# Dense stage of a four-layer residual kernel: separate PSUM banks per sum, 512-column products, outputs put together on VectorE

## The chip, the core and the metric

The kernel runs on one core of a Trainium2 chip. The metric is the device time of one execution in microseconds (us), the median of three runs. TensorE (PE) is the matrix engine and PEld its weight loads, VectorE is DVE, ScalarE is ACT, GpSimd is POOL and SyncE is SP.

## What is computed

x has 128 sequences of 64 channels and 1024 positions, in float32. Four layers follow each other, each added to its input:

```
x = x + L0(x)   # a long convolution of each channel, masked by the sequence's length
x = x + L1(x)   # each sequence: a 64x64 mix of the channels, one of 16 chosen by an index
x = x + L2(x)   # x @ W2.T + bias + (x @ A2.T) @ B2.T, the rank-16 pair A2, B2 one of 32
x = x + L3(x)   # x @ W3.T + 0.5 * (x @ A3) @ B3.T, rank 32, A3 one of 5
```

L2 and L3 work along the 1024 positions. The kernel multiplies their dense weights into one 1024 x 1024 matrix and keeps what is low in rank (both adapters and the bias) as a separate product of small rows.

## The kernel before

There are three stages. The preparation, to about 190 us, builds the combined weights and the tables. The convolution follows, to about 580 us. The **dense stage** does L1, L2 and L3, and the change lies there; outside it only the places of some weight columns move.

A tile is 128 rows: two sequences of 64 channels. The dense stage takes two tiles at a time, a **pair**: 32 pairs, of which the first and the last are written out and the rest run in a loop on every engine (`over_pairs`). A pair is a 2 x 2 block matrix a11, a12, a21, a22 (128 rows x 512 positions each), and the combined weight is 2 x 2 blocks of 512 x 512. Winograd's form of Strassen's method makes the four output blocks from seven products M1 to M7 instead of eight:

```
y11 = M1 + M2                  y12 = M1 + M6 + M5 + M3
y21 = M1 + M6 + M7 + M4        y22 = M1 + M6 + M7 + M5
```

The signs lie in the operands and weights, and all four take low-rank rows on top. Every operand is held as a high and a low part in a reduced format of float32, so a product is three passes over four chunks of 128 positions: 12 steps. A step of 512 output columns was issued as two matmuls of 256. M1, M5, M2 and M4 are **wide**: they also form 96 columns for the adapters (x times the A tables), so their two matmuls have 256 and 352 columns. M6, M3 and M7 are **plain**.

The order of a pair's work on TensorE is written out in `pair` of the tensor block: M1, M5, M2, M4 (with a transpose, `turn`, of the adapters' rows in its middle), `adapters` (a small product), a `quarter` (the L1 mix of a quarter of the next pair, eight matmuls at L1573), M6 with the second `turn` in its middle, `low_rank` for y11, `adapters`, a quarter, M3, a quarter, M7, three `low_rank`, the last quarter. Each `low_rank` is four matmuls of 256 columns, two accumulating steps for two halves. The engines' orders are fixed by hand as well; all waits are semaphores.

PSUM has 8 banks of 512 float32 columns. Before the change, two sums share a bank by halves: P (M1, then M6 and M7 added onto it) and S (M2) share one, R (M5, then M3) and V (M4) another (`PS_SHARED`, `RV_SHARED`). The rest:

- ScalarE copies sums out into `y_out` on the way: M1 (L1386), M5 (L1391), M1 + M6 after the first `low_rank` (L1395), M1 + M6 + M7 (L1404). The first two overwrite `y_out` of the previous pair and so wait for its two stores (`y_stored`).
- VectorE adds a second PSUM sum onto each: y11 (L1541), y12 (L1548), y22 (L1553), y21 (L1555). It also makes the operands of the next products (L1466 to L1470 xs1 and its parts, L1512 to L1523), chooses the next rows by sequence length (L1442, L1447) and gathers the adapters' columns (`h_rows`, L1481 and L1485, which adds the parts of two products; `h_columns`, L1490).
- ScalarE issues the stores of the output rows (L1408 first tile, L1415 second), SP the loads.
- M1 of the next pair waits for y22's addition, since it writes the bank of P.

```
L1621  pe.wait_ge(a11_lo, n + 1)
L1622  pe.wait_ge(h_lo[0], n + 1)
L1623  ready(pe, y22_added, n)
L1624  product(xa11, M1, PS_SHARED, P_OWN, ALL, True).then_inc(m1_done, 1)
```

Of the kernel before, what the change touches and what calls it, by code (L numbers as in the profile page):

```python
# [39 lines left out]
H_AT = (HB, 0, HB, 0)  # L40
D_AT = (0, KR, 0, KR)


def program(nc, x, xt_in, steps, cond, adapter, labeler, log_dt, ssm_c, log_a_real, a_imag, ssm_d,
# [276 lines left out]
    def count_in(k, u, bufs=BUFS):  # L321
# [30 lines left out]
    m1_done, m5_done, m2_done, m4_done, lr11_done, m7_done, rv_done, p_done = (  # L352
        sem(f"{n}_done") for n in ("m1", "m5", "m2", "m4", "lr11", "m7", "rv", "p"))
    p_copied, r_copied, u2_copied, u3_copied = (sem(f"{n}_copied") for n in ("p", "r", "u2", "u3"))
    h_part, hrow_ready, turned, hc_ready, adapted, hs_hi, hs_lo = (
        sem(n) for n in ("h_part", "hrow_ready", "turned", "hc_ready", "adapted", "hs_hi", "hs_lo"))
    y11_added, y12_added, y22_added, y21_added = (sem(f"{n}_added") for n in ("y11", "y12", "y22", "y21"))
# [908 lines left out]
    with nc.Block() as block:  # L1266
# [89 lines left out]
        def _(act):  # L1356
# [22 lines left out]
            def pair(n, last_one):  # L1379
# [6 lines left out]
                copy(halves(y_out[0][:, 0:HB]), of_p, ACT.Copy).then_inc(p_copied, 1)  # L1386
# [4 lines left out]
                copy(halves(y_out[1][:, HB:T]), of_r, ACT.Copy).then_inc(r_copied, 1)  # L1391
# [3 lines left out]
                copy(halves(y_out[0][:, HB:T]), of_p, ACT.Copy).then_inc(u2_copied, 1)  # L1395
# [164 lines left out]
        def _(pe):  # L1560
# [59 lines left out]
            def pair(n, last_one):  # L1620
# [44 lines left out]
                if not last_one:  # L1665
                    quarter(n + 1, 3)
# [41 lines left out]
```

## Time and profile before

| | |
|---|---|
| median of 3 runs | 1503.09 us (1501.48 to 1505.19) |
| the profiled execution: span | 1500.9 us, first to last instruction |
| TensorE busy | 1456.2 us, 97% |
| VectorE busy | 1114.5 us, 74% |
| ScalarE busy | 631.1 us, 42% |
| GpSimd busy | 117.3 us, 8% |
| granted TensorE clock, mean | 0.995 of 2.4 GHz |

The three runs are timed without the profiler; the profiled execution is known by its span. Busy shares are means over stages with different limits, and a busy TensorE is not one without stalls: matmuls are pipelined, so the record of one (about 280 ns for 256 columns) overlaps the next, and what a matmul costs is the time from its start to the next one's start.

### The profile page before, as it was taken

To read this page: it belongs to the slowest core of one execution; us is meant where nothing else is said; L and a number is where in the kernel's file an instruction comes from. 1 tells how busy PE (TensorE), PEld (TensorE's weight loads), DVE (VectorE), ACT (ScalarE), POOL (GpSimd) and SP (SyncE) were. 2 spreads that over 40 slices of the span, in tenths; PEclk is the share of its full clock that TensorE was granted. 3 is DMA by queue.
4 is the path that set the end of the run, shared out by engine and by line. 5 is a ranking of instruction groups with operands and counts; after the bars stand their busy time and mean duration, and the time that the engine had idled before them with its cause. 6 is when DMAs were issued, how large, how long until landed. Compare 5 with 4: busy or idle time off the path is not lost.

```text
span 1500.9 us, 33974 instructions
## 1 busy us (share of the span) xinstructions
PE 1456.2 (97%) x10624; PEld 1404.1 (94%) x10624; DVE 1114.5 (74%) x2330; ACT 631.1 (42%) x1249; POOL 117.3 (8%) x188
## 2 busy tenths in 40 slices
PE   6989989999999997999999999999999999999998
PEld 5877879999999997999999999999999999999998
DVE  7975388888888885777777777777777777777674
ACT  4331256665656562343343343343343343334332
POOL 3451210000000000000000000000000000000000
PEclk9999999999999998999999999999999999999999
DMA  8133168888888877456556556556556656645652
GB/s 306 33 134 99 42 220 277 274 277 273 274 272 274 273 242 228 128 158 198 146 157 196 145 163 191 145 160 195 142 151 193 160 147 179 177 147 166 191 147 78
DMA packets 121380, 276.16 MB, mean 184 GB/s; under 512 B 23897, under 2 KB 64349, under 8 KB 118689
## 3 DMA queue, kind: packets, MB, share of 16 engines
q1 hardware_dynamic: 111308, 241.28, 54.1%
q10 hardware_dynamic: 10038, 34.46, 5.8%
q8 instruction: 18, 0.29, 0.1%
q14 instruction: 16, 0.13, 0.0%
HBM read 200.72 MB, written 74.95 MB: 184 GB/s over the span
## 4 chain that ended last, share of the span: by engine, by line
PE 87%; DVE 6%; DMA 3%; POOL 1%; issue 1%; ACT 1%; SPq 0%; DVEq 0%; ACTq 0%; POOLq 0%
PE ps L1602 23%; PE ps L1603 23%; PE ps L1234 13%; PE ps L1573 8%; PE ps L1245 6%; PE ps L1136 4%; PE ps L1225 3%; PE ps L1610 2%; PE ps L1612 2%; PE ps L1237 2%; DMA out<-y_out 1%; PE ps L1584 1%; DVE p L810 1%; DVE b3t L906 1%; DMA b_d<-b_last 1%
## 5 line engine op out<-in xcount | busy, mean ns | idle before, releaser
L1602 PE MATMUL ps<-weights,xs 128*128 128x256 f32 x1536 | 397.4, 289 | 0.0
L1603 PE MATMUL ps<-weights,xs 128*128 128x256 f32 (+1 forms) x1536 | 388.8, 292 | 0.0
L1602 PE MATMUL ps<-weights,xa 128*128 128x352 f32 (+1 forms) x1152 | 329.2, 313 | 4.6 <-ACT y_out L1386 1.3
L1603 PE MATMUL ps<-weights,xa 128*128 128x256 f32 (+1 forms) x1152 | 322.7, 295 | 0.0
L1602 PEld LDWEIGHTS ps<-weights,xs 128*128 128x128 f32 x1536 | 292.5, 190 | 0.0
L1603 PEld LDWEIGHTS ps<-weights,xs 128*128 128x128 f32 x1536 | 292.4, 190 | 0.0
L1602 PEld LDWEIGHTS ps<-weights,xa 128*128 128x128 f32 x1152 | 217.0, 188 | 10.7 <-issue 10.7
L1234 PE MATMUL ps<-toep,ut 128*128 128x512 f32 (+2 forms) x1152 | 226.7, 342 | 0.0
L1603 PEld LDWEIGHTS ps<-weights,xa 128*128 128x128 f32 x1152 | 217.2, 189 | 0.0
L1234 PEld LDWEIGHTS ps<-toep,ut 128*128 128x128 f32 x1152 | 194.3, 189 | 16.6
L1362 ACT ACTIVATE a<-ps 128x512 f32<-128x512 f32 x128 | 76.5, 598 | 274.2 <-PE ps L1573 259.5
L1573 PE MATMUL ps<-m_gath,x_in 128*128 128x128 f32 x1024 | 137.2, 278 | 8.9 <-DVE x_in L1455 8.9
L1573 PEld LDWEIGHTS ps<-m_gath,x_in 128*128 128x128 f32 x1024 | 127.0, 195 | 9.3 <-DVE x_in L1455 9.3
L1136 PE MATMUL ps<-p,staged 128*128 128x512 f32 x480 | 111.2, 393 | 6.9 <-POOL staged L595 4.8
L752 ACT ACTIVATE ut<-xt 128x896 fp32r<-128x896 f32 x64 | 61.0, 953 | 135.2 <-PE ps L1245 129.2
L1136 PEld LDWEIGHTS ps<-p,staged 128*128 128x128 f32 x480 | 90.9, 190 | 26.7 <-issue 5.2
L1334 POOL COPY m_gath<-mix 64x64 f32 x128 | 46.1, 360 | 823.0 <-PE ps L1573 719.9
L1245 PE MATMUL ps<-toep,ut 128*128 128x256 f32 x768 | 107.3, 289 | 0.0
L1447 DVE COPY_PREDICATED x_in<-late,x_nat 128x512 f32<-128x512 uint16 x124 | 92.5, 746 | 18.9 <-DVE late L1442 18.9
L1245 PEld LDWEIGHTS ps<-toep,ut 128*128 128x128 f32 x768 | 95.8, 190 | 0.0
L422 ACT ACTIVATE weights<-tab 128x128 fp32r<-128x128 f32 (+1 forms) x256 | 71.4, 353 | 26.6 <-DVE tab L429 26.5
L1059 DVE TENSOR_TENSOR ut<-xt,ut 128x896 fp32r<-128x896 f32 x64 | 69.9, 1092 | 16.3 <-ACT ut L752 16.3
(223 smaller groups left out, 2182.3 us busy)
## 6 DMA issues: line engine op xcount, KB each, us to landing
lags<-kern_d SPq DMA_DIRECT2D x64, 512.0 KB, 5.2
xt<-in_xt SPq DMA_DIRECT2D x64, 512.0 KB, 6.0
x_d<-yo SPq DMA_DIRECT2D x64, 512.0 KB, 3.2
x_nat<-in_x SPq DMA_DIRECT2D x64, 512.0 KB, 3.9
x_in<-x_d SPq DMA_DIRECT2D x64, 512.0 KB, 5.6
out<-y_out ACTq DMA_DIRECT2D x63, 512.0 KB, 5.8
tab<-a_d SPq DMA_DIRECT2D x128, 128.0 KB, 2.1
stack<-b_d SPq DMA_DIRECT2D x126, 128.0 KB, 4.1
```

Source lines behind the costliest of these rows:

```text
L422: ins = nc.scalar.activation(to, of, ACT.Copy)
L752: copy(ut[u % 2][:, 0, 0:SPLIT], xt[u % BUFS][:, 0:SPLIT], ACT.Copy).then_inc(ut_hi, 1)
L1059: tt(ut[u % 2][:, 1, 0:SPLIT], xt[u % BUFS][:, 0:SPLIT], f(ut[u % 2][:, 0, 0:SPLIT]), ALU.subtract).then_inc(ut_lo, 1)
L1136: ins = mm(t[:, cols], staged[n % 2][:, a, c, :], p3[:, c, b, cols], start=c == a == b == 0, stop=c == K8 - 1 and a == 1)
L1234: mm(y[:, half * HB + i * P:(half + 1) * HB], xs[:, a, half * half_t + i, :], tp[:, b, 0:HB - i * P], start=i == a == b == 0, stop=False)
L1245: ins = mm(y[:, to:to + QT], xs[:, a, i, :], tp[:, b, at_col:at_col + QT], start=False, stop=i == half_t - 1 and a == 1)
L1334: ins = nc.gpsimd.tensor_copy(m_gath[v][rows, b * C:(b + 1) * C], mix[rows, bass.ds(s, 1), :].squeeze(1))
L1362: ins = copy(raw[:], mixing, ACT.Copy)
L1447: nc.vector.copy_predicated(x1_in[v][:, cols], late[:], x_nat[v][:, cols]).then_inc(chosen[v], 1)
L1573: ins = mm(acc[:, bank, i * P:(i + 1) * P], x1_in[v][:, c * P:(c + 1) * P], m_gath[v][:], start=True, stop=True)
L1602: mm(left[0], x_part, left[1], start=first and is_wide, stop=end, skip_group_check=True)
L1603: ins = mm(right[0], x_part, right[1], start=first and is_wide and H_AT[m] > 0, stop=end, skip_group_check=True)
```

## The change

- **PSUM banks.** Six banks for the sums of products, none shared: `S_LEFT`, `S_RIGHT` hold M1 and M2 (y11), `V_LEFT`, `V_RIGHT` hold M5 and M4, `P_BANK` M6 and then M7, `Q_BANK` M3. In S and V the 96 adapter columns stand behind the right half, so all four wide products run 256 then 352 columns (M2 and M4 were 352 then 256), and the adapters' columns of two products add up in PSUM: `h_rows` loses its additions.
- **Plain products** write one bank of 512 columns: one matmul of 512 for two of 256. The low-rank rows of y12 and y22 do the same.
- **Outputs.** ScalarE copies M1 (now S), M5 (now V) and later y11 as a whole. VectorE forms M1 - M5 and M1 + M5 from the copies (`pair_sums`) and adds P, V and Q to them from PSUM (V holds M5 + M4 by then, so y21 starts from M1 - M5). The two copies of U2 and U3 on ScalarE are gone.
- **Order and waits.** On TensorE the last quarter moves ahead of the last `low_rank`, which waits for VectorE's read of P after M7 (`u3_read`). M1 waits for y11's copy, M6 for y22, M3 for y12. ScalarE copies a12 without waiting for M7, and the second store waits for y22 as well as y21. In the last pair the y11 half is stored by itself.

The core of the diff, the banks first:

```diff
-    S_OWN, PS_SHARED, P_OWN, V_OWN, RV_SHARED, R_OWN, SMALL_BANK, MIX_BANK = range(8)
+    S_LEFT, S_RIGHT, V_LEFT, V_RIGHT, P_BANK, Q_BANK, SMALL_BANK, MIX_BANK = range(8)
```

ScalarE's part of a pair:

```diff
-                copy(halves(y_out[0][:, 0:HB]), of_p, ACT.Copy).then_inc(p_copied, 1)
+                copy(halves(y_out[0][:, 0:HB]), of_s, ACT.Copy).then_inc(m1_copied, 1)
...
-                copy(halves(y_out[1][:, HB:T]), of_r, ACT.Copy).then_inc(r_copied, 1)
+                copy(halves(y_out[1][:, HB:T]), of_v, ACT.Copy).then_inc(m5_copied, 1)
...
                 act.wait_ge(lr11_done, n + 1)
-                copy(halves(y_out[0][:, HB:T]), of_p, ACT.Copy).then_inc(u2_copied, 1)
+                act.wait_ge(pair_sums, 2 * n + 2)
+                copy(halves(y_out[0][:, 0:HB]), of_s, ACT.Copy).then_inc(y11_copied, 1)
...
-                act.wait_ge(m7_done, n + 1)
-                copy(halves(y_out[1][:, 0:HB]), of_p, ACT.Copy).then_inc(u3_copied, 1)
-                if not last_one:
                     take(n + 1, 3, a12, xa12)
                 act.wait_ge(y12_added, n + 1)
...
                 else:
+                    act.wait_ge(y22_added, n + 1)
                     act.dma_start(out_rows[bass.ds(2 * n + 1, 1)].squeeze(0), y_out[1][:]).then_inc(y_stored[1], 16)
```

VectorE's part:

```diff
+                dve.wait_ge(m1_copied, n + 1)
+                dve.wait_ge(m5_copied, n + 1)
+                tt(y_out[1][:, 0:HB], y_out[0][:, 0:HB], y_out[1][:, HB:T], ALU.subtract).then_inc(pair_sums, 1)
+                tt(y_out[1][:, HB:T], y_out[0][:, 0:HB], y_out[1][:, HB:T], ALU.add).then_inc(pair_sums, 1)
                 dve.wait_ge(m2_done, n + 1)
                 h_rows(n, 0)
...
-                dve.wait_ge(u2_copied, n + 1)
-                tt(halves(y_out[0][:, 0:HB]), halves(y_out[0][:, 0:HB]), of_s, ALU.add).then_inc(y11_added, 1)
+                dve.wait_ge(m6_done, n + 1)
+                dve.wait_ge(pair_sums, 2 * n + 2)
+                tt(y_out[0][:, HB:T], y_out[1][:, HB:T], of_p, ALU.add).then_inc(u2_read, 1)
```

TensorE, the plain products and the order of a pair:

```diff
+            def plain_product(operand, m, bank, chunks, opens):
+
+                for i in chunks:
+                    for a, b in PASSES:
+                        ins = mm(acc[:, bank], operand[:, a, i, :], plain(i, b, m), start=opens and i == a == b == 0,
+                                 stop=i == K4 - 1 and a == 1, skip_group_check=True)
+                return ins
...
+            PIECES_S = ((acc[:, S_LEFT, 0:HALF], HALF), (acc[:, S_RIGHT, 0:HALF], HALF))
+            PIECES_P, PIECES_Q = ((of_p, HB),), ((of_q, HB),)
...
-                ready(pe, y22_added, n)
-                product(xa11, M1, PS_SHARED, P_OWN, ALL, True).then_inc(m1_done, 1)
+                ready(pe, y11_copied, n)
+                wide_product(xa11, M1, S_LEFT, S_RIGHT, ALL, True).then_inc(m1_done, 1)
...
-                pe.wait_ge(y11_added, n + 1)
-                product(xs3, M7, PS_SHARED, P_OWN, ALL, False).then_inc(m7_done, 1)
-                low_rank(0, HB, acc[:, RV_SHARED, LEFT], acc[:, R_OWN, LEFT])
+                pe.wait_ge(u2_read, n + 1)
+                plain_product(xs3, M7, P_BANK, ALL, False).then_inc(m7_done, 1)
+                low_rank(0, HB, PIECES_Q)
...
-                low_rank(1, 0, acc[:, V_OWN, RIGHT], acc[:, RV_SHARED, RIGHT]).then_inc(rv_done, 1)
-                pe.wait_ge(u3_copied, n + 1)
-                low_rank(1, HB, acc[:, PS_SHARED, LEFT], acc[:, P_OWN, LEFT]).then_inc(p_done, 1)
+                low_rank(1, 0, PIECES_V).then_inc(qv_done, 1)
                 if not last_one:
                     quarter(n + 1, 3)
+                pe.wait_ge(u3_read, n + 1)
+                low_rank(1, HB, PIECES_P).then_inc(p_done, 1)
```

TensorE at the end of a pair, before (stack and hs are the low-rank operands, m_gath and x_in the quarter's, xa_157 the operand of M1):

```order
L1610 MATMUL ps<-stack_175,hs_182 128x256 [waits u3_copied]
L1612 MATMUL ps<-stack_175,hs_182 128x256
L1610 MATMUL ps<-stack_175,hs_182 128x256
L1612 MATMUL ps<-stack_175,hs_182 128x256
L1573 MATMUL ps<-m_gath_189,x_in_188 128x128 [waits quarter_read,chosen0]
L1573 MATMUL ps<-m_gath_189,x_in_188 128x128 x3
L368 UNCONDITIONAL_BRANCH
L368 ISA
L1602 MATMUL ps<-weights,xa_157 128x256 [waits y22_added,h_lo0,x_a11_lo]
```

The same place after the change:

```order
L1601 MATMUL ps<-weights,xs_163 128x512 x11
L1610 MATMUL ps<-stack_174,hs_181 128x512 x2
L1610 MATMUL ps<-stack_175,hs_182 128x256 [waits stack_landed1,hs_lo]
L1610 MATMUL ps<-stack_175,hs_182 128x256 x3
L1574 MATMUL ps<-m_gath_189,x_in_188 128x128 [waits quarter_read,chosen0]
L1574 MATMUL ps<-m_gath_189,x_in_188 128x128 x3
L1610 MATMUL ps<-stack_175,hs_182 128x512 [waits u3_read]
L1610 MATMUL ps<-stack_175,hs_182 128x512
L366 UNCONDITIONAL_BRANCH
L366 ISA
L1593 MATMUL ps<-weights,xa_157 128x256 [waits y11_copied,h_lo0,x_a11_lo]
```

The last low-rank rows stand behind the quarter instead of ahead of it, and M1 waits for y11's copy instead of y22's addition. M7 and two of the low-rank groups are matmuls of 512 columns.

VectorE ahead of the first transpose, before (late and x_in belong to the choice of the next rows, hrow is what TensorE transposes):

```order
L1442 TENSOR_SCALAR late<-ramp,lens_cols 128x256 [waits chosen0,x_landed0,x1_landed0]
L1442 TENSOR_SCALAR late<-ramp,lens_cols 128x256
L1447 COPY_PREDICATED x_in_188<-late,x_nat_177 128x512 [waits late_made]
L1481 COPY hrow_191<-ps 64x48 [waits m2_done]
L1481 COPY hrow_191<-ps 64x48
L1485 TENSOR_TENSOR hrow_191<-hrow_191,ps 64x48 [waits h_part]
L1485 TENSOR_TENSOR hrow_191<-hrow_191,ps 64x48
L1490 COPY hc_179<-ps 64x128 [waits turned]
```

and after:

```order
L1446 TENSOR_SCALAR late<-ramp,lens_cols 128x256 [waits chosen0,x_landed0,x1_landed0]
L1446 TENSOR_SCALAR late<-ramp,lens_cols 128x256
L1451 COPY_PREDICATED x_in_188<-late,x_nat_177 128x512 [waits late_made]
L1525 TENSOR_TENSOR y_out_173<-y_out_172,y_out_173 128x512 [waits m5_copied,m1_copied]
L1526 TENSOR_TENSOR y_out_173<-y_out_172,y_out_173 128x512
L1481 COPY hrow_191<-ps 64x48 [waits m2_done]
L1481 COPY hrow_191<-ps 64x48
L1486 COPY hc_179<-ps 64x128 [waits turned]
```

The two sums of copied products stand between the choice and the adapters' rows, and the rows' two additions are gone.

## Rows read from the trace of the kernel before

**Rows 1.** The page: busy time, share of the span, instructions of each engine.

```profile
PE 1456.2 (97%) x10624; PEld 1404.1 (94%) x10624; DVE 1114.5 (74%) x2330; ACT 631.1 (42%) x1249; POOL 117.3 (8%) x188
```

**Rows 2.** By stretches: length, engines' busy us, granted clock, DMA share, GB/s.

```profile
800.00:900.00 100.00, 99.70 (x792) 99.01 (x791) 73.08 (x183) 39.13 (x85) 4.49 (x12) 1.00 0.56 160
```

**Rows 3.** Timeline, TensorE, first M1 in pairs 1 and 31 (start, us).

```profile
615.64 0.35 PE L1602 MATMUL ps<-weights,xa 128*128 128x256 f32 x1
...
1470.88 0.35 PE L1602 MATMUL ps<-weights,xa 128*128 128x256 f32 x1
```

**Rows 4.** Timeline, TensorE: a quarter, then M7 (second and following matmuls).

```profile
809.28 1.06 PE L1573 MATMUL ps<-m_gath,x_in 128*128 128x128 f32 x8
...
810.30 0.28 PE L1603 MATMUL ps<-weights,xs 128*128 128x256 f32 x1
...
813.05 0.28 PE L1610 MATMUL ps<-stack,hs 128*128 128x256 f32 x1
```

**Rows 5.** Timeline, TensorE in the preparation, equal matmuls merged.

```profile
120.91 65.57 PE L1136 MATMUL ps<-p,staged 128*128 128x512 f32 x288 [0.60 <-DVE lora_out L1025]
```

**Rows 6.** Groups by line and form, TensorE, 512 columns (busy us, mean ns).

```profile
L1234 PE MATMUL ps<-toep,ut 128*128 128x512 f32 x384 | 115.1, 407 | 0.0
L1136 PE MATMUL ps<-p,staged 128*128 128x512 f32 x480 | 111.2, 393 | 6.9 <-POOL staged L595 4.8 <-DVE raw L932 1.6 <-DVE lora_out L1025 0.6
```

**Rows 7.** Timeline, VectorE and TensorE, end of the pair before 815.64.

```profile
812.88 0.69 DVE L1470 TENSOR_TENSOR xs<-s,xs 128x512 fp32r<-128x512 f32 x1
814.21 0.69 DVE L1548 TENSOR_TENSOR y_out<-y_out,ps 128x512 f32<-128x512 f32 x1 [0.63 <-PE ps L1612]
814.48 1.06 PE L1573 MATMUL ps<-m_gath,x_in 128*128 128x128 f32 x8
814.81 0.68 DVE L1553 TENSOR_TENSOR y_out<-y_out,ps 128x512 f32<-128x512 f32 x1
...
815.83 0.33 PE L1603 MATMUL ps<-weights,xa 128*128 128x352 f32 x1
```

**Rows 8.** Timeline, ScalarE, the next pair: copies of M1, M5 and M1 + M6.

```profile
821.04 0.60 ACT L1386 ACTIVATE y_out<-ps 128x512 f32<-128x512 f32 x1 [1.74 <-DMA out<-y_out]
...
824.44 0.60 ACT L1391 ACTIVATE y_out<-ps 128x512 f32<-128x512 f32 x1 [2.28 <-DMA out<-y_out]
...
833.88 0.60 ACT L1395 ACTIVATE y_out<-ps 128x512 f32<-128x512 f32 x1 [2.37 <-PE ps L1612]
```

**Rows 9.** Timeline, TensorE, the same pair: steps of M1, then M2 into M4.

```profile
816.00 0.28 PE L1602 MATMUL ps<-weights,xa 128*128 128x256 f32 x1
...
816.55 0.28 PE L1602 MATMUL ps<-weights,xa 128*128 128x256 f32 x1
...
825.37 0.32 PE L1602 MATMUL ps<-weights,xa 128*128 128x352 f32 x1
...
825.65 0.32 PE L1602 MATMUL ps<-weights,xa 128*128 128x352 f32 x1
```

**Rows 10.** Timeline, VectorE and TensorE, the same pair, up to the first transpose (L1579).

```profile
824.85 0.75 DVE L1447 COPY_PREDICATED x_in<-late,x_nat 128x512 f32<-128x512 uint16 x1 [0.15 <-DVE late L1442]
825.85 0.42 DVE L1481 COPY hrow<-ps 64x48 f32<-64x48 f32 x2 [0.25 <-PE ps L1603]
826.31 0.41 DVE L1485 TENSOR_TENSOR hrow<-hrow,ps 64x48 f32<-64x48 f32 x2
...
827.33 0.27 PE L1579 MATMUL ps<-ident,hrow 128*128 128x128 f32 x1
```

**Rows 11.** By line: landing of the first store (L1408), then the second (L1415).

```profile
DMA to landing us min/median/max: 2.7/5.3/5.9
...
DMA to landing us min/median/max: 5.8/7.6/8.9
```

**Rows 12.** Timeline, a late pair: M5's copy on ScalarE, then M4 on TensorE.

```profile
1451.67 0.60 ACT L1391 ACTIVATE y_out<-ps 128x512 f32<-128x512 f32 x1 [2.85 <-DMA out<-y_out]
...
1452.41 0.40 PE L1602 MATMUL ps<-weights,xa 128*128 128x352 f32 x1 [0.25 <-ACT y_out L1391]
```

More of the change, by code:

```diff
@@ L351, in program @@
     h_hi, h_lo = [sem(f"h_hi{v}") for v in range(2)], [sem(f"h_lo{v}") for v in range(2)]
[L352 to L357, printed above, removed]
+    m1_done, m5_done, m2_done, m4_done, m6_done, lr11_done, m7_done, qv_done, p_done = (
+        sem(f"{n}_done") for n in ("m1", "m5", "m2", "m4", "m6", "lr11", "m7", "qv", "p"))
+    m1_copied, m5_copied, y11_copied = (sem(f"{n}_copied") for n in ("m1", "m5", "y11"))
+    hrow_ready, turned, hc_ready, adapted, hs_hi, hs_lo = (
+        sem(n) for n in ("hrow_ready", "turned", "hc_ready", "adapted", "hs_hi", "hs_lo"))
+    pair_sums, u2_read, u3_read = sem("pair_sums"), sem("u2_read"), sem("u3_read")
+    y12_added, y22_added, y21_added = (sem(f"{n}_added") for n in ("y12", "y22", "y21"))
     PAIRS = TILES // 2
@@ L373, in h_table @@
     def h_table(half, m):
-        start = (half * 4 + m) * WIDE + H_AT[m]
+        start = (half * 4 + m) * WIDE + HB
         cols = weights[:, :, start:start + KR]
@@ L1472, in h_rows @@
             def h_rows(n, v):
-                own, other = ((P_OWN, H_END), (S_OWN, H_FRONT)) if v == 0 else ((R_OWN, H_END), (V_OWN, H_FRONT))
-                parts = []
+                bank = (S_RIGHT, V_RIGHT)[v]
                 for b in range(2):
-                    rows, cols = slice(b * C, (b + 1) * C), slice(b * R2, b * R2 + R2 + R3)
-                    parts.append((hrow[v][rows, cols], rows, slice(b * (R2 + R3), (b + 1) * (R2 + R3))))
-                first, second = acc[:, own[0], own[1]], acc[:, other[0], other[1]]
-                for b, (to, rows, cols) in enumerate(parts):
-                    ins = nc.vector.tensor_copy(to, first[rows, cols])
-                ins.then_inc(h_part, 1)
-                dve.wait_ge(h_part, 2 * n + v + 1)
-                for to, rows, cols in parts:
-                    ins = tt(to, to, second[rows, cols], ALU.add)
+                    rows, start = slice(b * C, (b + 1) * C), H_COLS + b * (R2 + R3)
+                    ins = nc.vector.tensor_copy(hrow[v][rows, b * R2:b * R2 + R2 + R3], acc[rows, bank, start:start + R2 + R3])
                 ins.then_inc(hrow_ready, 1)
@@ L1584, in adapters, with wide_product @@
                 mm(acc[:, SMALL_BANK, P:2 * P], c_gath[v][:], hc[v][:], start=True, stop=True).then_inc(adapted, 1)
[L1586 removed]
+            def wide_product(operand, m, left, right, chunks, opens):
                 for i in chunks:
                     for a, b in PASSES:
[L1590 to L1603 removed]
@@ new lines, in wide_product @@
+                        start, end = opens and i == a == b == 0, i == K4 - 1 and a == 1
+                        x_part, w = operand[:, a, i, :], wide(i, b, m)
+                        mm(acc[:, left, 0:HALF], x_part, w[:, 0:HALF], start=start, stop=end, skip_group_check=True)
+                        ins = mm(acc[:, right, 0:HALF + KR], x_part, w[:, HALF:WIDE], start=start, stop=end, skip_group_check=True)
+                return ins
[4 more added lines that the diff above has]
+                                 stop=i == K4 - 1 and a == 1, skip_group_check=True)
+                return ins
```

93 lines of the change are left out of this document (42 added, 51 removed).

## Prediction

> **What bounds the kernel now.** I read the page's engine totals, then the table by stretches, then single instructions. TensorE is busy 97% of the span [rows 1], and in the dense stage, from 614 us on, over 99% at full clock, with VectorE at 73% and ScalarE at 39% [rows 2]. One turn of the dense loop (a pair) takes (1470.88 - 615.64) / 30 = 28.51 us [rows 3]. So the time there is the length of TensorE's instruction stream plus its stalls, and work on other engines counts only where TensorE waits for it. The duration in a row of a matmul is latency, since matmuls overlap; what counts is start to start. Two things in the stream can be shortened: the 256-column matmuls of M6, M3 and M7 with their low-rank rows, and one stall at each pair's end, which the busy share hides.
>
> **The merge of 256 to 512 columns.** From 810.30 to 813.05 stand 23 matmuls of 256 columns of M7, so one takes 2.75 / 23 = 119.6 ns [rows 4]. The kernel has matmuls of 512 columns in the same arithmetic, accumulating into one bank, in its preparation: 288 in 65.57 us, less some 0.17 us of latency of the last, give 227.1 ns each [rows 5]. Two of 256 cost 239.1 ns, so a merge saves 12 ns. A pair merges 36 in M6, M3 and M7 and 4 in the low-rank additions: 40 x 12 = 0.48 us, times 32 pairs = **15.4 us**. The convolution's matmuls of 512 columns have a mean record of 407 ns against 393 ns in the preparation [rows 6]; read as 14 ns more of pitch, this would be 241 ns, and the merge would gain nothing. That is the lower end, 0; I take 15.4 because the preparation's rows have the same passes and the same width into one bank. The Trainium skill (TensorE: Matmul & The Clock Gate, Back-to-back issue gap) puts the isolated spacing at N/2.4 + 2.5 ns, by which a merge would save only 2.5 ns, some 3 us in all; the trace does not agree at 256 columns, where the page would have 109.2 ns and the rows have 119.6.
>
> **The stall at the pair's end.** Inside a pair, from the first matmul of a quarter (eight matmuls at L1573) to the second matmul of the next product is 810.30 - 809.28 = 1.02 us [rows 4]; at the pair's end it is 815.83 - 814.48 = 1.35 us [rows 7]. The 0.33 us more are a wait: M1 waits for y22's addition (L1553), which ends at 814.81 + 0.68 = 815.49 [rows 7]. The change lets M1 wait for y11's copy, which follows lr11, some 10 us earlier (a copy stands at that place now, at 833.88 [rows 8], in a pair that ends at 844), and y22's bank is first needed at M6. So the wait goes: 0.33 x 31 pair ends = **10.2 us**. What is late next there is M5, which waits for y21; VectorE adds it within about 1 us of the pair's end, and M5 comes a whole M1, 3.3 us, after it.
>
> **M2 and M4 in the other order.** They now run 256 then 352 columns, as M1 and M5 do. At M4's start two matmuls take 0.28 us (825.37 to 825.65), in this pair's M1 four take 0.55 (816.00 to 816.55) [rows 9]. Gain per pair between 0 (the spacing is the pair's, not the order's) and 24 x 4.5 ns = 0.11 us, in all 0 to 3.5 us; nothing in these rows favours an end, so I take the middle, **1.7 us**.
>
> **What VectorE gets more.** Two sums (M1 - M5, M1 + M5) and one more addition of y, at about 0.60 us start to start [rows 7], less two additions of 0.2 us for each of two h_rows [rows 10]: +1.8 - 0.8 = 1.0 us per pair, on an engine idle 27%. It costs only where TensorE waits.
>
> (a) *The first transpose (turn 0), in the middle of M4.* The sums stand ahead of h_rows, and both behind the choice of the next rows, in VectorE's queue. That queue hangs on the landing of the previous pair's first store: landing at 821.04 (ScalarE's copy of M1 starts, and behind it that of xs3, for which VectorE waits), the second choice ends at 824.85 + 0.75 = 825.60, 4.56 us after the landing; now h_rows starts at 825.85 because it waits for M2 [rows 8, 10]. After the change: sums from about 825.64, 0.60 + 0.69 = 1.28 us, to 826.92; two copies 0.42, started 0.08 before the sum's end, to 827.26; 0.14 us more until TensorE moves (1451.67 + 0.60 to 1452.41 in a pair that waited for a copy [rows 12]): 827.40, that is 6.36 us after the landing. TensorE wants it at 827.33 [rows 10]. Counted from M1's second matmul (815.83) that is 11.50, less up to 0.08 for the new order of M2 and M4. The landing: in ScalarE's program the first store still follows quarter 3's copies, and quarter 3 moves ahead of the last low-rank rows (2 x 0.227 = 0.45 us in place of the 0.33 of stall), so it comes 0.12 us earlier in this frame: 821.04 - 815.83 - 0.12 = 5.09, plus 6.36 = 11.45 against 11.42 to 11.50. The slack of about half a us that the turn has now is used up. Landings scatter (2.7 to 5.9 us after issue, median 5.3 [rows 11]), so some pairs wait and some don't: I take 0.1 us per pair, **-3 us**, between 0 and 0.4 (-12).
>
> (b) *The last low-rank rows of a pair* wait for VectorE's read of U3. VectorE is free after xs1 low at about 813.50 (L1470, [rows 7]) and done at 814.19; TensorE gets there at 813.05 - 0.15 (M7 shorter) + 0.45 + 0.48 + 0.89 (low-rank rows, low-rank rows, quarter) = 814.7. Cover 0.4 us with the start-up: cost nothing. Without it, up to 0.4 us per pair.
>
> (c) *M4's start* waits for the copy of M5 into y_out[1], and that for the second store. Here the copy ends at 824.44 + 0.60 = 825.04 [rows 8], M4 starts at 825.65 [rows 9]: slack 0.47 with the 0.14. After the change the second store waits for y22's addition (0.69 us), which can begin only when the last low-rank rows are out, about when M1 begins, where now M1 begins behind it [rows 7]: by the two additions' places some 0.4 us later in the pair. Landing is 7.6 us after issue in the median, 8.9 at most [rows 11]. Both stores are in ScalarE's queue, and the first lands only 5 us after issue, so a later second one mostly loses waiting time behind it: cost nothing, bound 0.4 us per pair.
>
> ScalarE loses one copy of 0.60 us per pair; it has idle time at each, so nothing. The preparation's moved columns have equal sizes: nothing. **Tail:** the last pair's y11 half is stored ahead, so less is left to move at the end, but VectorE has one more addition (0.60 us) behind M7. Between -0.6 and +0.6 us; I take 0.
>
> **Sum:** 15.4 + 10.2 + 1.7 - 3 = 24.3 us. The profiled execution's span is 1500.9 us, so the span becomes 1476.6. The median of the runs, 1503.09, lies 2.2 above this span (the lowest 0.6, the highest 4.3), so I forecast 1503.1 - 24.3 = **1478.8 us**, about 1.6% faster. About 0.3% (4.5 us) is what a measurement of this kernel can tell from no change.
>
> **Rivals.**
> 1. *The merge gains little.* The fixed part of a matmul grows with its width, as the convolution's longer records hint. Then only 10.2 + 1.7 - 3 = 9 us stay: 1494. Against it: 288 matmuls at 227.1 ns. Chance 0.08, of which 0.03 for a saving of about a fifth of mine, 12 us in all, 1491. The page named above would have about this latter time.
> 2. *Turn 0 waits in nearly every pair*, 0.5 us each (landings as late as 5.7 to 5.9 us, the sums slower than additions from PSUM): 3 becomes 15.5 us, 1491. For it: the slack is used up by my own count. Against: a late landing also delays M4 in the same pairs, which then shares the wait. Chance 0.10.
> 3. *The change trades the stall for another at the same place*: the last low-rank rows wait for U3's read as long as M1 did for y22. 10.2 us go: 1489. Chance 0.06.
> 4. *The second store becomes the bound: slower.* Its issue moves behind y22, the copy of M5 comes late, and M4, both sums and turn 0 wait for it in every pair. Slower than 1507.6 needs a stall of (24.3 + 4.5) / 31 = 0.93 us per pair beyond what I count; with the slack of 0.47 the copy of M5 must come 1.4 us later than now against M4, when 0.4 comes from the issue. So the median landing would have to rise from 7.6 by 1.0 to 8.6 us after issue, close to the worst of 31 now. At 2 us of stall per pair it is 1503 + 38 = 1541. For it: in [rows 12] this very wait already stops TensorE once. Chance 0.06.
>
> **How the numbers follow.** My forecast has 0.70, its own range 1471 (M2 and M4 at their full 3.5 us, no wait at turn 0, the tail's 0.6, and 2 us for the scatter of the runs) to 1490 (0.4 us at turn 0 and the same 2 us). With rival 3 and half of rival 2, which lie within, the range 1471 to 1490 holds about 0.8. Faster by over 0.3%: forecast 0.70, rival 1 0.07, rival 2 0.07, rival 3 0.04, together 0.88. Within 0.3%: the worse ends of rivals 1 to 3, 0.05. Slower: rival 4 and the same waits added up, 0.07.
>
> **What would show it.** Spacing of the 512-column matmuls in M6, M3 and M7 near 227 ns; no gap between the last low-rank rows and M1; a pair of about 27.7 us; TensorE records about 10624 - 32 x 40 = 9344; gaps of 0 to 0.4 us at turn 0, with the low-rank rows and M4 following without any. Wrong: spacing of 235 ns or more, a pair over 28.1 us, or regular waits of M4 for the copy of M5.

## The result, and the profile after

The changed kernel takes **1480.52 us** (median of 4 runs, 1480.08 to 1481.02) against 1502.96 (4 runs) before: ratio 0.9848, 95% interval 0.9834 to 0.9862, 22.4 us faster. The forecast was 1478.8. The profiled execution spans 1478.4 us (before 1500.9).

Totals of the page, to read against [rows 1], and the same 100 us as in [rows 2]:

```profile
PE 1434.4 (97%) x9344; PEld 1330.9 (90%) x9344; DVE 1140.7 (77%) x2298; ACT 612.5 (41%) x1217; POOL 119.0 (8%) x188
```
```profile
800.00:900.00 100.00, 100.00 (x654) 93.11 (x653) 78.64 (x183) 38.74 (x85) 5.20 (x14) 1.00 0.55 166
```

TensorE has 1280 records less; in these 100 us it is still busy all the time, at full clock. What has changed is the length of its stream. The first M1 of the second and of the last pair, against [rows 3]:

```profile
617.94 0.29 PE L1593 MATMUL ps<-weights,xa 128*128 128x256 f32 x1
...
1450.02 0.29 PE L1593 MATMUL ps<-weights,xa 128*128 128x256 f32 x1
```

A pair takes 832.08 / 30 = 27.74 us in the mean (28.51 before) and 27.64 from the fourth on; the second and third take 29.0. To see where a pair's time goes, the table cuts it at matmul starts in the trace: mean us over the fifth to the thirtieth pair, in the kernel before, in the changed one and in three runs told of below (halves: the merge undone; quarter back and wait only: one half each of the new order at the pair's end undone).

| stretch, to the next one's start | before | after | halves | quarter back | wait only |
|---|---|---|---|---|---|
| M1 | 3.400 | 3.292 | 3.363 | 3.398 | 3.402 |
| M5 | 3.320 | 3.280 | 3.360 | 3.316 | 3.323 |
| M2 | 3.364 | 3.321 | 3.279 | 3.330 | 3.298 |
| M4, turn 0 in its middle | 3.470 | 3.472 | 3.424 | 3.601 | 3.433 |
| adapters, quarters 0 and 1 | 2.069 | 2.067 | 2.066 | 2.066 | 2.067 |
| M6, turn 1, y11's low-rank rows | 3.535 | 3.445 | 3.527 | 3.445 | 3.447 |
| M3, quarter 2 | 3.770 | 3.647 | 3.770 | 3.647 | 3.648 |
| M7 | 2.954 | 2.818 | 2.954 | 2.817 | 2.817 |
| low-rank rows of Q and V | 0.959 | 0.935 | 0.961 | 1.657 | 0.935 |
| quarter 3, last low-rank rows, wait at M1 | 1.633 | 1.364 | 1.373 | 1.384 | 2.400 |
| sum | 28.47 | 27.64 | 28.08 | 28.66 | 28.77 |

Three groups of rows give 0.831 of the 0.833 us per pair: the merged products and low-rank rows 0.373 (0.090 + 0.123 + 0.136 + 0.024), the pair's end with M1 behind it 0.377 (0.269 + 0.108), and M5, M2 and M4 0.081.

The stretch that answers to [rows 4] and [rows 7], TensorE's timeline from quarter 2 to the next M1:

```profile
835.70 1.05 PE L1574 MATMUL ps<-m_gath,x_in 128*128 128x128 f32 x8
836.51 2.98 PE L1601 MATMUL ps<-weights,xs 128*128 128x512 f32 x12
839.33 1.10 PE L1610 MATMUL ps<-stack,hs 128*128 128x512 f32 x6
840.26 1.05 PE L1574 MATMUL ps<-m_gath,x_in 128*128 128x128 f32 x8
841.07 0.72 PE L1610 MATMUL ps<-stack,hs 128*128 128x512 f32 x2
841.62 0.29 PE L1593 MATMUL ps<-weights,xa 128*128 128x256 f32 x1
```

M7 is 12 matmuls in 2.82 us, and M1 starts 0.55 us after the first of the last two low-rank matmuls: no gap. By their single starts in the trace, M7's 12 take 314, 232, 231 and nine times 226 or 227 ns. The 24 of 256 before took 202, 118, 119, 121, 117, 117 and then 120 each. So a merge saves 240 - 227 = 13 ns far from the quarter, but only 6, 8 and 3 ns in the first three (320 - 314, 240 - 232, 234 - 231). An estimate by the isolated gap of the Trainium skill (TensorE: Matmul & The Clock Gate, Back-to-back issue gap), N/2.4 + 2.5 ns, is 215.8 ns at 512 columns; the trace does not agree at this width either, the rows have 227.

VectorE at the end of the same pair, against [rows 7]: the last of the next pair's sums, then the read of U3 (the bank P after M7), for which the last low-rank rows wait:

```profile
839.30 0.69 DVE L1474 TENSOR_TENSOR xs<-s,xs 128x512 fp32r<-128x512 f32 x1
839.91 0.68 DVE L1549 TENSOR_TENSOR y_out<-y_out,ps 128x512 f32<-128x512 f32 x1
```

The read ends 1.26 us after M7 (840.59 - 839.33), and the rows that wait for it start at 841.07.

VectorE and TensorE up to turn 0 in the next pair, against [rows 10]:

```profile
851.76 0.69 DVE L1526 TENSOR_TENSOR y_out<-y_out,y_out 128x512 f32<-128x512 f32 x1
...
852.36 0.42 DVE L1481 COPY hrow<-ps 64x48 f32<-64x48 f32 x2
...
853.18 0.27 PE L1580 MATMUL ps<-ident,hrow 128*128 128x128 f32 x1
```

The sums run and h_rows follows them without idle time; the copies end at 852.78, with 0.14 of start-up at 852.92, and TensorE asks at 853.18. That is 0.26 us of slack. What was not forecast stands in the second and third pairs. ScalarE's copies of M1 (L1384) and M5 (L1389) wait for the stores there:

```profile
618.91 0.37 ACTq L1419 DMA_DIRECT2D out<-y_out  x1
...
627.81 0.60 ACT L1389 ACTIVATE y_out<-ps 128x512 f32<-128x512 f32 x1 [4.17 <-DMA out<-y_out]
...
647.08 0.37 ACTq L1411 DMA_DIRECT2D out<-y_out  x1
...
653.70 0.60 ACT L1384 ACTIVATE y_out<-ps 128x512 f32<-128x512 f32 x1 [3.07 <-DMA out<-y_out]
```

and TensorE waits for those copies, one row from each of the two pairs:

```profile
628.55 0.36 PE L1593 MATMUL ps<-weights,xa 128*128 128x256 f32 x1 [0.56 <-ACT y_out L1389]
...
654.44 0.36 PE L1593 MATMUL ps<-weights,xa 128*128 128x256 f32 x1 [0.70 <-ACT y_out L1384]
```

### The profile page after: what moved, and what is told of

The parts are those of the page before. It is cut to its first block, busy times and chain, and to the rows that moved or that the text cites. A ratio compares the mean times of both kernels' runs of the same rounds, so it can differ in the third digit from the quotient of the medians.

```text
span 1478.4 us, 31603 instructions
## 1 busy us (share of the span) xinstructions
PE 1434.4 (97%) x9344; PEld 1330.9 (90%) x9344; DVE 1140.7 (77%) x2298; ACT 612.5 (41%) x1217; POOL 119.0 (8%) x188
## 4 chain that ended last, share of the span: by engine, by line
PE 86%; DVE 7%; DMA 3%; POOL 1%; issue 1%; ACT 1%; SPq 0%; DVEq 0%; ACTq 0%; POOLq 0%
PE ps L1601 18%; PE ps L1594 15%; PE ps L1232 13%; PE ps L1593 11%; PE ps L1574 8%; PE ps L1243 6%; PE ps L1134 4%; PE ps L1610 4%; PE ps L1223 3%; PE ps L1235 2%; DMA out<-y_out 1%; PE ps L1585 1%; DVE p L808 1%; DVE b3t L904 1%; DMA b_d<-b_last 1%
## 5 line engine op out<-in xcount | busy, mean ns | idle before, releaser
L1593 PE MATMUL ps<-weights,xa 128*128 128x256 f32 x1152 | 321.8, 282 | 2.3 <-ACT y_out L1384 1.6
L1594 PE MATMUL ps<-weights,xa 128*128 128x352 f32 x1152 | 322.7, 322 | 0.0
L1601 PE MATMUL ps<-weights,xs 128*128 128x512 f32 x1152 | 291.2, 401 | 0.0
L1601 PEld LDWEIGHTS ps<-weights,xs 128*128 128x128 f32 x1152 | 207.0, 189 | 40.4
L1594 PE MATMUL ps<-weights,xs 128*128 128x352 f32 x384 | 106.4, 320 | 0.0
L1593 PE MATMUL ps<-weights,xs 128*128 128x256 f32 x384 | 105.1, 278 | 0.0
```

The source lines that it names most:

```text
L1593: mm(acc[:, left, 0:HALF], x_part, w[:, 0:HALF], start=start, stop=end, skip_group_check=True)
L1594: ins = mm(acc[:, right, 0:HALF + KR], x_part, w[:, HALF:WIDE], start=start, stop=end, skip_group_check=True)
L1601: ins = mm(acc[:, bank], operand[:, a, i, :], plain(i, b, m), start=opens and i == a == b == 0, stop=i == K4 - 1 and a == 1, skip_group_ch ...
```

## The experiments

Each run is the changed kernel with one edit, timed beside the kernel before on the same chip. The dense stage here is the time from the first matmul of M1 to the last matmul of the trace; a pair is the mean of the fifth to the thirtieth.

| run | median us | ratio to before (95%) | dense stage us | pair us |
|---|---|---|---|---|
| kernel before (profile) | | | 910.1 | 28.47 |
| changed kernel | 1480.5 | 0.985 (0.983 to 0.986) | 885.4 | 27.64 |
| the same again | 1479.2 | 0.983 (0.982 to 0.984) | 886.1 | 27.64 |
| halves | 1491.5 | 0.992 (0.990 to 0.993) | 896.4 | 28.08 |
| quarter back | 1510.2 | 1.003 (1.002 to 1.005) | 917.3 | 28.66 |
| wait only | 1512.5 | 1.006 (1.004 to 1.007) | 918.5 | 28.77 |
| stall back | 1511.7 | 1.005 (1.004 to 1.006) | 914.3 | 28.60 |
| all back | 1511.3 | 1.005 (1.004 to 1.007) | 916.5 | 28.66 |
| U3 first | 1565.0 | 1.040 (1.038 to 1.042) | 970.7 | 30.46 |
| extra sum | 1491.5 | 0.991 (0.989 to 0.992) | 898.9 | 28.01 |
| sums late | 1480.7 | 0.983 (0.981 to 0.985) | 885.4 | 27.65 |
| wide swap | 1484.5 | 0.987 (0.985 to 0.988) | 890.4 | 27.78 |
| half stores | 1476.8 | 0.981 (0.980 to 0.982) | 883.0 | 27.64 |
| half stores again | 1478.6 | 0.983 (0.981 to 0.984) | 882.8 | 27.64 |

**Halves.**

```diff
-                        ins = mm(acc[:, bank], operand[:, a, i, :], plain(i, b, m), start=opens and i == a == b == 0,
+                        for cols in (slice(0, HALF), slice(HALF, HB)):
+                            ins = mm(acc[:, bank, cols], operand[:, a, i, :], plain(i, b, m)[:, cols],
...
-            PIECES_P, PIECES_Q = ((of_p, HB),), ((of_q, HB),)
+            PIECES_P = ((of_p[:, 0:HALF], HALF), (of_p[:, HALF:HB], HALF))
```

> The changed kernel, with its plain products (M6, M3, M7) and the low-rank rows of P and Q issued as two matmuls of 256 columns into the same bank; nothing else goes back. Theory: the merge is worth what its segments show between the two traces, 0.37 to 0.39 us a pair, so this run is 12 to 13 us above 1480.5, at 1492 to 1494; if the prediction's 12 ns per merge holds in full, 15.4 us, 1496. Rival, the merge gains little and the gain lies in the order and the banks: 1481 to 1484. Spacing of the 256-column matmuls: 119 to 120 ns.

Measured 1491.5 us, ratio 0.9915, which is 0.7 to 0.9% above the changed kernel: 10 to 13 us. (This run computes wrong sums in M6 and M3, where each half of a bank is opened with a start mark of its own. Its instructions and their shapes are as described, and the run with all back, whose sums are right, has the same 2.954 us for M7.) M6, M3, M7 and the low-rank rows, those at the pair's end among them (0.009), go back by 0.376 us a pair, all that they had lost. TensorE, quarter 2 and M7:

```profile
835.86 3.12 PE L1602 MATMUL ps<-weights,xs 128*128 128x256 f32 x24
838.82 1.05 PE L1574 MATMUL ps<-m_gath,x_in 128*128 128x128 f32 x8
839.63 3.12 PE L1602 MATMUL ps<-weights,xs 128*128 128x256 f32 x24
842.58 1.12 PE L1611 MATMUL ps<-stack,hs 128*128 128x256 f32 x8
```

M7 takes 842.58 - 839.63 = 2.95 us, 2.82 as 12 of 512. The rival in the expectation (the merge gains little) falls: the merge is worth 0.376 x 32 = 12.0 us. The other 0.06 us of the longer pair lie in the wide products, which this edit does not touch (M1 and M5 +0.15, M2 and M4 -0.09).

**Quarter back.**

```diff
-                if not last_one:
-                    quarter(n + 1, 3)
                 pe.wait_ge(u3_read, n + 1)
                 low_rank(1, HB, PIECES_P).then_inc(p_done, 1)
+                if not last_one:
+                    quarter(n + 1, 3)
```

> The changed kernel with quarter 3 back behind the last low-rank rows; M1 still waits for y11's copy alone. Theory (the prediction's step b): the read of U3 is covered by the quarter, and with the quarter gone from there the last low-rank rows wait about 0.4 us in each pair: 12 us more, 1490 to 1495, with the gap in front of L1610's last rows. Rival, the quarter's place is worth nothing, because only the wait of M1 for y22 made the stall: 1480 to 1482.

Measured 1510.2 us: 28 to 30 us more, over twice what was expected, and slower than the kernel before. The pair's end in this run, VectorE and TensorE:

```profile
902.61 2.44 DVE L436 TENSOR_TENSOR weights<-tab,weights 128x128 fp32r<-128x128 f32 x8
...
904.96 0.68 DVE L1470 TENSOR_TENSOR s<-a,a 128x512 f32<-128x512 f32 x1
905.56 0.68 DVE L1471 TENSOR_TENSOR xa<-a,xa 128x512 fp32r<-128x512 f32 x1
905.67 1.10 PE L1610 MATMUL ps<-stack,hs 128*128 128x512 f32 x6
...
906.34 0.69 DVE L1474 TENSOR_TENSOR xs<-s,xs 128x512 fp32r<-128x512 f32 x1
906.95 0.68 DVE L1549 TENSOR_TENSOR y_out<-y_out,ps 128x512 f32<-128x512 f32 x1
...
907.69 0.74 PE L1610 MATMUL ps<-stack,hs 128*128 128x512 f32 x2 [0.92 <-DVE y_out L1549]
```

M7 ends at 905.67, but U3's read (L1549) starts at 906.95, behind VectorE's table work (L436) and the next pair's sums (L1470 to L1474), without idle time between. The last low-rank rows come 0.74 us behind it. In the mean the wait is 1.657 - 0.935 = 0.72 us, not 0.4, and M1 and turn 0 lose another 0.11 and 0.13. Part of the 0.72 is that VectorE's chain comes later in this run: its table work waits longer for the load of the tables (1.6 us in the mean, 1.05 in the changed kernel), and the sums end 1.01 us after M7 instead of 0.67. TensorE's row in the table of waits, of this run, then of the changed kernel (us in all, times, longest):

```profile
PE ps L1610 <- DVE y_out L1549: 17.3, 31, 1.6
```
```profile
PE ps L1610 <- DVE y_out L1549: 0.3, 1, 0.3
```

**Wait only.**

```diff
-                ready(pe, y11_copied, n)
+                ready(pe, y22_added, n)
                 wide_product(xa11, M1, S_LEFT, S_RIGHT, ALL, True).then_inc(m1_done, 1)
...
```

M6 waits for y11's copy in exchange, and VectorE adds y22 ahead of y21.

> The changed kernel with M1 waiting for y22's addition as before, but quarter 3 left ahead of the last low-rank rows; y22 is added ahead of y21. Theory: nothing stands between the last low-rank rows and M1 now, so the whole addition shows, 0.85 to 0.9 us a pair: 26 to 28 us, 1507 to 1509, slower than the kernel before. Rival (the wait is worth 0.33 us wherever the quarter stands): 10 us, 1491.

Measured 1512.5 us, a little above the expected 1507 to 1509: the last stretch is 1.04 us longer, and M1 loses 0.11. In the timeline y22's addition (named L1554 in this kernel) runs with nothing beside it on TensorE:

```profile
904.63 0.72 PE L1610 MATMUL ps<-stack,hs 128*128 128x512 f32 x2
...
905.39 0.69 DVE L1554 TENSOR_TENSOR y_out<-y_out,ps 128x512 f32<-128x512 f32 x1 [0.64 <-PE ps L1610]
...
906.22 0.35 PE L1593 MATMUL ps<-weights,xa 128*128 128x256 f32 x1 [0.87 <-DVE y_out L1554]
```

So neither half of the new order at the pair's end is worth anything alone. With the quarter ahead and the old wait, or with the new wait and the quarter behind, the kernel is slower than before; the gain exists only with both.

**Stall back**: both edits at once, and y22 added ahead of y21, as in the run above. The last of the three is shown.

```diff
-                tt(halves(y_out[1][:, 0:HB]), halves(y_out[1][:, 0:HB]), of_v, ALU.add).then_inc(y21_added, 1)
                 dve.wait_ge(p_done, n + 1)
                 tt(y_out[1][:, HB:T], y_out[1][:, HB:T], of_p, ALU.add).then_inc(y22_added, 1)
+                tt(halves(y_out[1][:, 0:HB]), halves(y_out[1][:, 0:HB]), of_v, ALU.add).then_inc(y21_added, 1)
```

> The changed kernel with the pair's end as it was: quarter 3 behind the last low-rank rows, M1 waiting for y22's addition, and y22 added ahead of y21 on VectorE. Theory: VectorE's chain U3, y12, y22 sets the pair's end, and the stall of 0.33 us in each pair of the kernel before comes back, here with the U3 read in it: 0.35 to 0.55 us a pair, 11 to 17 us, 1491 to 1498. Rival, the stall was not worth its gap (what TensorE loses there it makes up elsewhere): 1481 to 1485.

Measured 1511.7 us, twice the expected loss, for the reason seen in the run with the quarter alone: the last low-rank rows wait for U3 (the stretch of Q's and V's low-rank rows takes 1.461 us), and M1 waits 0.22 us (quarter 3 takes 1.034 us to M1, 0.812 without a wait). The old order doesn't give the old time back: before the change U3 was read by a copy on ScalarE (L1404), not behind VectorE's sums.

**All back**: the edits above and the halves (but for one matmul of 512 at the start of each sum).

```diff
+                        start = opens and i == a == b == 0
+                        for cols in (slice(0, HB),) if start else (slice(0, HALF), slice(HALF, HB)):
...
```

> The changed kernel with three things back at once: the plain products in halves of 256 columns (the first matmul of a product excepted, 34 of 36 in a pair), quarter 3 behind the last low-rank rows, and M1 waiting for y22, which is added ahead of y21. Theory: the parts add up, 11 us for the halves and 29 for the pair's end by the dense spans of those two runs: dense stage 923 to 927 us against 910 in the kernel before, some 15 us slower than that; what is left of the change (U3 read by VectorE behind its sums, where a copy of ScalarE read it) costs that. Rival: longer products give VectorE the time it lacks at the pair's end, so the two cover each other: dense stage 910 to 916, about the time of the kernel before.

Measured 1511.3 us, dense stage 916.5: the halves cost next to nothing on top of the late pair's end (0.06 us a pair, 2.2 us of dense stage). The longer products give VectorE time, so the wait for U3 shrinks: that stretch is 1.212 us here, 1.461 above. The two do not add up. Against the kernel before a pair is 0.19 us longer (28.66 against 28.47), and the stretch with the wait for U3 alone has 0.253 more (1.212 against 0.959): in these pairs the wait for U3 is what stays (0.5% of the time).

**U3 first**: the quarter back as above, and U3 read ahead of the sums, which is the part shown.

```diff
                     h_low(dve, n + 1, 1)
-                    sums(n + 1)
                 dve.wait_ge(m7_done, n + 1)
                 tt(y_out[1][:, 0:HB], y_out[1][:, 0:HB], of_p, ALU.add).then_inc(u3_read, 1)
+                if not last_one:
+                    sums(n + 1)
```

> The changed kernel with quarter 3 back behind the last low-rank rows, and VectorE's read of U3 put ahead of the next pair's three sums (L1470 to L1474) instead of behind them. Theory: in the run with quarter 3 alone put back, the last low-rank rows waited because VectorE still had those sums to do when M7 ended; read first, U3 is out 0.83 us after M7 while Q's and V's low-rank rows take 0.93: the 0.4 to 0.75 us of wait ahead of the last low-rank rows go, their stretch from M7's end is 0.93 to 1.0 us against 1.3 to 1.7. Rival: the read takes too long by itself, and the stretch stays above 1.3 us. In the time as a whole the later sums delay quarter 3's copies and the first store behind them, so M4 and turn 0 may wait more: between 10 us below that run and 20 above.

The expected part came: the stretch is 0.942 us, so the order of VectorE's queue made that wait. The price was far above the guess: 1565.0 us. The sums end later, so xs1 and quarter 3's copies on ScalarE do, and the first store behind them: it is issued 1.31 us after M1's start in the median (0.47 in the run with the quarter alone). It also takes longer, 6.6 us from issue to landing where that run has 5.2. ScalarE, then the TensorE row that follows:

```profile
924.16 0.59 ACT L1362 ACTIVATE xa<-ps 128x512 fp32r<-128x512 f32 x1
924.69 0.34 ACTq L1411 DMA_DIRECT2D out<-y_out  x1
...
931.28 0.60 ACT L1384 ACTIVATE y_out<-ps 128x512 f32<-128x512 f32 x1 [3.04 <-DMA out<-y_out]
```
```profile
932.02 0.36 PE L1594 MATMUL ps<-weights,xa 128*128 128x256 f32 x1 [1.82 <-ACT y_out L1384]
```

M2 waits 1.82 us for M1's copy, and that for the store. Over the run this one wait is the largest on TensorE:

```profile
PE ps L1594 <- ACT y_out L1384: 56.7, 31, 4.1
```

This is the mechanism of the prediction's rival 4, with the first store in place of the second.

**Extra sum.**

```diff
                 dve.wait_ge(m5_copied, n + 1)
+                tt(y_out[0][:, HB:T], y_out[0][:, 0:HB], y_out[1][:, HB:T], ALU.add)
                 tt(y_out[1][:, 0:HB], y_out[0][:, 0:HB], y_out[1][:, HB:T], ALU.subtract).then_inc(pair_sums, 1)
```

> The changed kernel with one more sum of 128x512 on VectorE, into a place that is overwritten later, just ahead of the two sums: 0.60 us more ahead of turn 0. By the prediction's count the slack there is used up already, so all of it shows: 0.6 us a pair, 18 us, ratio 0.996 to 0.998. By the trace of the changed kernel the transpose comes 0.3 us (median) after it could: 0.25 to 0.3 us a pair, 8 to 10 us, ratio 0.990 to 0.992. Rival, VectorE is off the path there: nothing.

Ratio 0.9908, some 9 to 12 us above the changed kernel; M4 with turn 0 takes 3.84 us against 3.47, 0.37 a pair of the 0.60 added. The slack was about 0.23 us, near the 0.26 of the row above. In its timeline TensorE now waits there:

```profile
941.12 0.42 DVE L1481 COPY hrow<-ps 64x48 f32<-64x48 f32 x2
941.59 0.33 PE L1581 MATMUL ps<-ident,hrow 128*128 128x128 f32 x1 [0.30 <-DVE hrow L1481]
```

**Sums late**: the sums and their waits (S) moved behind the first adapter rows.

```diff
-                S
                 dve.wait_ge(m2_done, n + 1)
                 h_rows(n, 0)
                 h_columns(n, 0)
+                S
```

> The changed kernel with VectorE's two sums (M1 - M5, M1 + M5) behind the first h_rows and h_columns instead of ahead of them. Theory: turn 0 waits for VectorE in a handful of pairs only, so little is left to win: 0 to 1 us less, ratio 0.984 to 0.985, with turn 0 at 0.16 us behind the matmul ahead of it in every pair. Rival (the prediction's term of 0.1 us per pair, 3 us, or its rival of 0.5 us): 3 us less or more, 0.983 or below.

Ratio 0.983, dense stage 885.4, as in the changed kernel. M4 with turn 0 takes 3.456 us, 0.016 less, and M6's stretch 0.026 more: nothing is left to win at turn 0.

**Wide swap.**

```diff
-                        mm(acc[:, left, 0:HALF], x_part, w[:, 0:HALF], start=start, stop=end, skip_group_check=True)
                         ins = mm(acc[:, right, 0:HALF + KR], x_part, w[:, HALF:WIDE], start=start, stop=end, skip_group_check=True)
+                        ins = mm(acc[:, left, 0:HALF], x_part, w[:, 0:HALF], start=start, stop=end, skip_group_check=True)
```

> The changed kernel with each step of the four wide products (M1, M5, M2, M4) issuing its 352 columns first and its 256 behind. Theory (the prediction's term for M2 and M4, 1.7 us in the middle of 0 to 3.5): the order of the two widths sets the step, 0.28 us with 352 first and 0.273 with 256 first; then M1 and M5 grow from 3.28 to 3.36 us, M2 and M4 by 0.03 to 0.08 each: 0.2 to 0.3 us a pair, 7 to 10 us, ratio to the kernel before 0.989 to 0.992. Rival: the two speeds come in either order (the kernel before has M1 and M5 at both, all with 256 first), so nothing: 0.984 to 0.986.

Between the two: the dense stage is 4 to 5 us longer, M1 takes 3.37 and M5 3.36 us (3.29 and 3.28 in the changed kernel), while M2 (3.32) and M4 (3.46, 3.47 there) hardly move. So the order is not what sets M2 and M4. M5 takes 3.28 or 3.36 us in the kernel before as well, 13 times each in the fifth to the thirtieth pair, with 256 first in all; in the halves it is 3.36 in all. What picks the speed was not found, so a few us between two of these runs need not be the edit's.

**The same again, and half stores**: the changed kernel once more, and one with four stores of half a row in a pair, profiled twice. In it y11's half is stored after its copy, M5 is copied into y21's half, and every half waits for its own store.

```diff
-                ready(act, y_stored[1], 16 * n)
-                copy(halves(y_out[1][:, HB:T]), of_v, ACT.Copy).then_inc(m5_copied, 1)
+                ready(act, y21_stored, 16 * n)
+                copy(halves(y_out[1][:, 0:HB]), of_v, ACT.Copy).then_inc(m5_copied, 1)
...
+                act.wait_ge(y11_copied, n + 1)
+                store(n, 0, 0, y11_stored)
```

> The changed kernel with four stores of half a row each in a pair in place of two: y11's half goes out behind its copy, M5 is copied into y21's half, and each half waits for its own store alone (the sums for y22's, the U2 addition for y12's). Theory: the first three pairs of the changed kernel are 1.3 us longer (29.0 against 27.64) because the copies of M1 and M5 wait for whole stores that land late, and that goes; the steady pairs stay at 27.64: 2 to 3 us less, ratio 0.982 to 0.984. Rival: late landings of what those pairs load, not the stores, make them long: no change, 0.984 to 0.986. If issuing two more stores on ScalarE's queue delays its copies: more, above 0.986.

> The changed kernel as it is, beside the two above and the one below on the same chip: 1479 to 1483 us, ratio 0.983 to 0.987. Its profile shows whether the long first pairs (29.0 us) and the dense stage's start (588.6 us) come back: if the start scatters between 586.8 and 590.9 as in the runs so far, the 2.9 us by which it was later than in the kernel before are nothing of the change.

> The kernel with four half stores once more, beside the changed kernel on the same chip. Theory: 3 to 6 us below it, from first pairs without waits for whole stores: pairs 2 and 3 at 27.6 to 27.8 us. Rival: the difference between the two earlier calls was the chip's: within 1.5 us of it.

In the profiles the theory holds: the second and the third pair take 27.64 us each in the second profile of the half stores, 29.5 and 28.9 in the changed kernel run beside it, and the dense stage is 2.4 to 3.3 us shorter. M1's copy in the third pair no longer waits for a store (the row at 653.70 above):

```profile
650.05 0.60 ACT L1388 ACTIVATE y_out<-ps 128x512 f32<-128x512 f32 x1
```

In the times it can't be told: 1478.56 against 1479.22 side by side, intervals 0.9813 to 0.9840 and 0.9817 to 0.9844. It is no slower, and nothing more is claimed.

## Why the prediction was right, step by step

The forecast for the time and for what bounds the kernel held. Its terms did less well than their sum: two misses of about 3 us, the merge and turn 0, cancel, and that the sum came so near is in part luck.

- **The merge**: 15.4 forecast, 12.0 measured (halves). The mechanism was right; the size failed at "Two of 256 cost 239.1 ns, so a merge saves 12 ns", which took the spacing of long unbroken runs ([rows 4, 5]) for all 40 merges. M6 is two runs of 6 behind a quarter and a transpose, M3 and M7 one of 12 behind a quarter, and the first three merges of each save little (3 to 8 ns in the M7 shown). The 14 ns of the convolution's records ([rows 6]) meant nothing for these.
- **The stall at the pair's end**: 10.2 forecast, 10.4 measured. The last stretch is 0.269 us shorter, and M1's first step (its first two matmuls) 0.068 (354 to 286 ns; with the quarter back, without a wait there, it is 364, so it is slow behind a quarter): together 0.337 x 31. The wait is gone, and the size was right. But the text gave the gain to M1's new wait and counted the quarter's move as a cover of 0.4 us under (b). The runs show that neither carries it alone: without the move the pair loses 1.0 us (quarter back), without the new wait 1.1 (wait only). For the changed kernel (b) was right: it puts the end of U3's read 1.29 us after M7 (814.19 against 813.05 - 0.15), and the rows have 1.26. The bound "Without it, up to 0.4 us per pair" was the weakest number of the prediction. It left VectorE's sums where they were, and with the quarter back they end later themselves; it also left out what M1 and turn 0 lose.
- **M2 and M4 in the other order**: 1.7 forecast; M2 gave 0.043 x 32 = 1.4 us, M4 nothing. M5, which the change leaves as it is, gave 1.3 more by the unexplained choice of speed, and M1 as much again (its steps behind the first went from 277 to 273 ns, 0.04 us in all); no term has these 2.6 us. The swap shows that order was not the reason, so this term was right by luck.
- **Turn 0**: -3 forecast, about 0 measured. The step "The slack of about half a us that the turn has now is used up" was 0.23 to 0.26 us too pessimistic. From M1's second matmul (841.75 us) the copies with start-up end 11.17 us later, not 11.45; M1's copy started (846.73) after 4.98, not 5.09, and VectorE's chain took 6.19, not 6.36.
- **(c) The stores**: nothing in steady pairs, as said. The second store is issued 0.4 us later against M1's start, as counted, and lands 6.8 us after issue in the median (7.6 in [rows 11]). Not foreseen: the second and third pairs are 2.7 us over two steady ones, where the kernel before was 0.5 over its own. That is 2.2 us lost, and the half stores show that these waits were the cause.
- **The tail**: 0 +- 0.6 forecast; from the start of the last matmul to the end 4.45 us against 5.06, 0.6 less.

Together the dense stage lost 910.1 - 885.4 = 24.7 us by the trace against 24.3 forecast: the merge came 3.4 short, turn 0 was 3 better, and most of what M1 and M5 gave by their speed was lost in the first pairs. The profile as a whole lost 22.5, since this execution began the dense stage at 588.6 us and the one before at 585.7. The profiles of the twelve runs begin it between 586.8 and 590.9, with nothing ahead of it changed, so a start this late is usual for these kernels. Whether the one profile of before was early by chance stays open. Timed beside the kernel before a second time, the changed kernel was 24.4 us faster (1479.22 against 1503.65).

**The rivals.** Rival 1 (the merge gains little) falls with the halves. Rival 2 (turn 0 waits in every pair) falls with the extra sum, which needed 0.23 us to bring it about, and with the sums late. Rival 3 (the stall traded for one at the last low-rank rows) is what happens as soon as the quarter goes back, at 0.72 us a pair rather than 0.33: it was nearer than its 0.06 says. Rival 4 does not hold here, but its mechanism is real: with U3 first, M2 waits 1.8 us in each pair for a copy that waits for a store.

## What to carry over

Price a moved instruction by the queue of the engine that answers it: the read of U3 takes 0.68 us, but it starts where VectorE's program order lets it, and 0.8 us of other work on TensorE ahead of the matmuls that wait for it was the difference between 1.5% faster and 0.3% slower. Take the gain of wider matmuls from rows of as many in succession as the kernel has, with their first matmuls behind whatever stands ahead of them. And do not undo half of a reordering that looks like two edits: here either half alone made the kernel slower than before.

## What the runs showed of the hardware that was not expected

In the run with U3 first, TensorE's granted clock fell after the wait of 1.82 us ahead of M2, although it had been at full clock and busy before it. By stretches (length, busy us of PE, PEld, DVE, ACT, POOL, granted clock, DMA share, GB/s):

```profile
928.20:930.20 2.00, 2.00 (x15) 1.75 (x13) 1.23 (x2) 0.04 (x1) 0.07 (x1) 1.00 0.93 354
930.20:932.00 1.80, 0.00 (x1) 0.01 (x1) 0.00 (x0) 0.72 (x2) 0.00 (x0) 1.00 1.05 394
932.00:934.00 2.00, 1.98 (x10) 2.00 (x10) 1.42 (x4) 0.40 (x1) 0.00 (x0) 0.62 1.10 248
934.00:936.00 2.00, 2.00 (x10) 2.00 (x10) 1.81 (x5) 0.60 (x1) 0.00 (x0) 0.52 0.56 84
936.00:938.00 2.00, 2.00 (x17) 2.00 (x16) 1.39 (x4) 0.00 (x0) 0.00 (x0) 1.00 0.00 0
```

At 0.52 of 2.4 GHz, about the lower of its two levels (1.2 GHz), ten matmuls run in 2 us, and 17 in the 2 us behind them. M2 takes 4.95 to 4.99 us in 8 of the 31 pairs that wait, in all eight at a granted clock of 0.50 to 0.53 from its first to its third us, and about 3.4 to 3.7 in the others. So such a wait costs another 1.5 us now and then. What sets the eight apart was not found. No pair of the kernel before or of the changed one stands still so long in its steady part.
